# A vision block with a state scan, on one core: wider products on GpSimd, small steps moved to other engines, slots planned anew

## The reference, cut to what matters

```python
xb = silu(causal_conv4(x @ in_proj_w[:512].T)); z = x @ in_proj_w[512:].T
dt, B, C = softplus(dt_w * p0 + dt_b), p[1:17], p[17:33]      # p = xb @ x_proj_w.T
dA = exp(dt * A);  xs = (xb * dt) * B                         # 512 channels x 16 states x 196 tokens
h[t] = dA[t] * h[t-1] + xs[t]                                 # associative_scan
y = sum_n(h[n] * C[n]) + xb * D
y = layernorm(y) * ln_g + ln_b
out = (y * silu(z)) @ out_w.T
```

## Time and profile before

| what | us |
|---|---|
| median of the 3 runs (5220.89 to 5222.7) | 5221.56 |
| the profiled execution | 5220.4 |
| its span, first to last instruction | 5218.4 |
| TensorE busy (92%) | 4818.3 |
| GpSimd busy (83%) | 4331.2 |
| VectorE busy (72%) | 3737.0 |
| ScalarE busy (71%) | 3699.1 |

### The profile page before, as it was taken

The page is one execution under the profiler, slowest core; times in us unless marked ns, Lnnn a source line. Parts: engine busy times, 40 slices in busy tenths (PEclk is TensorE's granted clock), DMA queues, the critical chain, the costliest instruction groups (busy, mean ns, idle before and its releaser), DMA issues. The chain is left out here.

```text
span 5218.4 us, 95840 instructions
## 1 busy us (share of the span) xinstructions
PE 4818.3 (92%) x33664; PEld 4253.9 (82%) x33664; DVE 3737.0 (72%) x7504; ACT 3699.1 (71%) x8898; POOL 4331.2 (83%) x3272
## 2 busy tenths in 40 slices
PE   4799999999999999999999999999999999999986
PEld 4678888888888888888888888888888888888776
DVE  3677777777777777777777777777777777777753
ACT  4687777777777777777777777777777777777741
POOL 4998888888888888888888898898898888888840
PEclk8899999999999999999999999999999999999986
DMA  4222222222222222222222222322222322322200
GB/s 98 61 62 65 65 64 65 68 61 64 68 62 64 70 62 62 70 61 63 67 62 64 70 62 62 71 61 62 72 60 61 76 59 59 76 59 59 67 17 25
DMA packets 730622, 329.01 MB, mean 63 GB/s; under 512 B 631542, under 2 KB 655392, under 8 KB 729888
## 3 DMA queue, kind: packets, MB, share of 16 engines
q1 hardware_dynamic: 730144, 322.89, 25.4%
HBM read 307.88 MB, written 14.90 MB: 62 GB/s over the span
## 5 line engine op out<-in xcount | busy, mean ns | idle before, releaser
L1087 DVE TENSOR_TENSOR_SCAN X<-dA,X 128x392 f32<-128x392 f32 x2048 | 1871.7, 956 | 727.2 <-POOL X L470 455.5
L470 POOL TENSOR_TENSOR X<-u,Bb 128x784 f32<-128x784 f32 x1024 | 1896.6, 1852 | 9.4 <-DMA Bb<-proj_rows 9.4
L480 POOL TENSOR_TENSOR X<-X,Cb 128x784 f32<-128x784 f32 x1024 | 1893.0, 1849 | 0.0
L890 ACT ACTIVATE dA<-dt,negA 128x195 f32<-128x195 f32 x4096 | 1512.4, 417 | 149.5 <-DVE X L1087 129.4
L597 PE MATMUL YB<-idn,X 128*98 128x128 f32 x8192 | 1108.3, 282 | 27.6 <-POOL X L480 27.6
L597 PEld LDWEIGHTS YB<-idn,X 128*98 128x98 f32 x8192 | 930.6, 132 | 63.5 <-POOL X L480 34.9
L717 PE MATMUL G<-hg,we 128*128 128x196 f32 x4096 | 739.1, 338 | 14.1 <-DVE hg L1203 14.1
L717 PEld LDWEIGHTS G<-hg,we 128*128 128x128 f32 x4096 | 714.2, 198 | 27.5 <-issue 19.6
L544 PE MATMUL YB<-win,idn 128*98 128x196 f32 x2176 | 444.1, 346 | 0.0
L689 PEld LDWEIGHTS G<-vs,pT 98*98 98x98 f32 x4096 | 391.6, 171 | 37.1 <-issue 34.3
L485 POOL TENSOR_TENSOR veps_att<-mv_att,epsc 98x2 f32<-98x2 f32 x64 | 12.5, 195 | 488.3 <-DVE mv_att L1096 488.3
(11 more groups left out here) (145 smaller groups left out, 7307.0 us busy)
## 6 DMA issues: line engine op xcount, KB each, us to landing
Bb<-proj_rows SPq DMA_DIRECT2D x256, 392.0 KB, 5.0
Cb<-proj_rows SPq DMA_DIRECT2D x256, 392.0 KB, 4.1
Gb<-gate_rows SPq DMA_DIRECT2D x64, 784.0 KB, 5.6
px<-in_x SPq DMA_DIRECT2D x1024, 36.8 KB
out<-ob SPq DMA_DIRECT2D x64, 196.0 KB
dtin<-proj_rows SPq DMA_DIRECT2D x64, 98.0 KB, 2.8
we<-in_w_e SPq DMA_DIRECT2D x1, 2048.0 KB
proj_rows<-pj SPq DMA_DIRECT2D x64, 25.3 KB
```

Of the source, the lines that this page charges most:

```text
L470: tt(X[(GROUPS * s + g) % RING][:], u[q % 2][:, c:c + 1, :].broadcast_to([P, NG, T]), Bb[:, NG * ng:NG * (ng + 1), :], ALU.mult).then_inc( ...
L480: tt(t[:], t[:], Cb[:, n0:n0 + NG, :], ALU.mult).then_inc(prod_ready, 1)
L890: last = go(dA[i % DRING][:, j, 1:T], dt_[q % 2][:, c, 1:T], ACT.Exp, scale=negA[:, c, n:n + 1])
L1087: v.tensor_tensor_scan(t, dA[i % DRING].rearrange("p n t -> p (n t)"), t, 0.0, ALU.mult, ALU.add).then_inc(scan_done, 1)
```

## The change

Products with B and C take eight states (`NW`) at once, 128 x 1568, in a ring of four tiles. The scan still goes by groups of four states, two to a tile. A product with C waits for both of its groups; the sums come at slot g+3. The gate of y goes to VectorE (`gate_y`), with `scale_y` writing in place in PSUM; the square goes to ScalarE; adding epsilon (at the end of `moments`) and the shift (`negative_mean`) go to VectorE, and only the power stays on GpSimd. All slots, the orders within a slot on all five queues and the assignment of uses to the shared banks are new. The fills are 3 matmuls an image instead of 17.

```diff
-RING = 6
+NW = 2 * NG
+WC = STATES // NW
+WIDES = IC * WC
+RING = 4
-AT_WARM = (5, 8, 9, 12, 13,)
-WARM = (4, 4, 4, 3, 2,)
-AT_LOAD = -39
+AT_WARM = (6, 11, 16, 6, 6,)
+WARM = (2, 0, 0, 0, 1,)
+AT_LOAD = -51
-AT_XPROJ_OUT = -14
-AT_PROJ_STORE = -12
-AT_DT_LOAD = -11
-AT_SOFT = -9
+AT_XPROJ_OUT = -15
+AT_PROJ_STORE = -23
+AT_DT_LOAD = -20
+AT_SOFT = -10
-AT_IN = -1
+AT_IN = -2
+AT_SUM = 3
-AT_B = (-4, -4, -1, -1,)
-AT_C = (-1, -3, 3, 0,)
+AT_B = (-15, -16, -14, -12,)
+AT_C = (-10, -7, -5, -6,)
-AT_Y_STD = 21
-AT_Y_NORM = 21
+AT_Y_STD = 19
+AT_Y_SHIFT = 20
+AT_Y_NORM = 22
-AT_Y3 = 25
-AT_OUT = 25
+AT_Y3 = 23
+AT_OUT = 26
+AT_FFN_SHIFT = 40
-AT_ATT_STD = 61
+AT_ATT_STD = 62
+AT_ATT_SHIFT = 62
-AT_GATE_STORE = 71
-AT_GATE_LOAD = 74
+AT_GATE_STORE = 61
+AT_GATE_LOAD = 63
...
-        X = [sb(f"X{i}", [P, NG, T]) for i in range(RING)]
+        X = [sb(f"X{i}", [P, NW, T]) for i in range(RING)]
...
+            def inputs(s, q, w):
+                c, n0 = w // WC, NW * (w % WC)
+                if w == 0:
                     pool.wait_ge(u_ready, s + 1)
                 if c == 0:
-                    pool.wait_ge(B_landed[ng], 16 * (s + 1))
-                after(pool, prod_used, GROUPS * s + g + 1 - RING)
+                    for ng in range(n0 // NG, (n0 + NW) // NG):
+                        pool.wait_ge(B_landed[ng], 16 * (s + 1))
+                after(pool, prod_used, GROUPS * s + 2 * (w + 1 - RING))
+                tt(X[(WIDES * s + w) % RING][:], u[q % 2][:, c:c + 1, :].broadcast_to([P, NW, T]), Bb[:, n0:n0 + NW, :],
                    ALU.mult).then_inc(xs_pool, 1)
+            def times_c(s, w):
+                n0 = NW * (w % WC)
+                pool.wait_ge(scan_done, 2 * (GROUPS * s + 2 * (w + 1)))
...
+                t = X[(WIDES * s + w) % RING]
+                tt(t[:], t[:], Cb[:, n0:n0 + NW, :], ALU.mult).then_inc(prod_ready, 1)
             def inverse_std(s, n):
-                pool.wait_ge(stats_step[n], 4 * (s + 1))
-                steps = 3 if n in shift else 2
-                tt(veps[n][:], mv[n][:, :, 1], epsc[:], ALU.add).then_inc(rstd_step[n], 1)
-                if n in shift:
-                    tt(shift[n][:], mv[n][:, :, 0], mone[:], ALU.mult).then_inc(rstd_step[n], 1)
-                pool.wait_ge(rstd_step[n], steps * (s + 1) - 1)
-                tt(rstd[n][:], veps[n][:], mhalf[:], ALU.pow).then_inc(rstd_step[n], 1)
-                if n in shift:
-                    pool.wait_ge(rstd_step[n], steps * (s + 1))
-                    tt(shift[n][:], shift[n][:], rstd[n][:], ALU.mult).then_inc(shifted[n], 1)
+                pool.wait_ge(veps_ready[n], s + 1)
+                tt(rstd[n][:], veps[n][:], mhalf[:], ALU.pow).then_inc(rstd_ready[n], 1)
...
-                    for s, q in at(AT_KSQ):
-                        pool.wait_ge(where["k"].drained, where["k"].count("k", s))
-                        tt(ka[:], ka[:], ka[:], ALU.mult).then_inc(ksq_ready, 1)
-                    for s, q in at(AT_Y3):
-                        pool.wait_ge(S.drained, S.count("turn_y", s))
-                        pool.wait_ge(S.drained, S.count("z", s))
-                        tt(y3[:], y3[:], zs[:], ALU.mult).then_inc(y3_ready, 1)
+                    for k in range(WIDES):
+                        for s, q in at(2 * k + AT_TIMES):
+                            times_c(s, k)
+                    for k in range(WIDES):
+                        for s, q in at(2 * k + AT_IN):
+                            inputs(s, q, k)
...
             def scale_y(s):
                 o = filled("turn_y", s)
                 for c in range(IC):
-                    last = go(y3[:, c, :], o[:, c // 2, (c % 2) * T:(c % 2 + 1) * T], ACT.Identity,
-                              scale=lng[:, c:c + 1], bias=lnb[:, c:c + 1])
-                last.then_inc(S.drained, 1)
+                    mine = o[:, c // 2, (c % 2) * T:(c % 2 + 1) * T]
+                    last = go(mine, mine, ACT.Identity, scale=lng[:, c:c + 1], bias=lnb[:, c:c + 1])
+                last.then_inc(y_scaled, 1)
...
+                    for s, q in at(AT_KSQ):
+                        act.wait_ge(where["k"].drained, where["k"].count("k", s))
+                        go(ka[:], ka[:], ACT.Square).then_inc(ksq_ready, 1)
...
+            def gate_y(s):
+                dve.wait_ge(y_scaled, s + 1)
+                dve.wait_ge(S.drained, S.count("z", s))
+                if s > 0:
+                    filled("out", s - 1)
+                v.tensor_tensor(y3[:].rearrange("p (a b) t -> p a (b t)", a=2), S.tile,
+                                zs[:].rearrange("p (a b) t -> p a (b t)", a=2), ALU.mult).then_inc(S.drained, 1)
+                dve.wait_ge(S.drained, S.count("turn_y", s))
+                dve.sem_inc(y3_ready, 1)
             def scan_group(s, g):
-                dve.wait_ge(xs_pool, GROUPS * s + g + 1)
+                dve.wait_ge(xs_pool, WIDES * s + g // 2 + 1)
...
+                dve.wait_ge(stats_step[n], 4 * s + 2 * BLK)
+                v.tensor_scalar(veps[n][:], mv[n][:, :, 1], LN_EPS, None, ALU.add).then_inc(veps_ready[n], 1)
+            def negative_mean(s, n):
+                dve.wait_ge(rstd_ready[n], s + 1)
+                v.scalar_tensor_tensor(out=shift[n][:], in0=mv[n][:, :, 0], scalar=-1.0, in1=rstd[n][:], op0=ALU.mult,
+                                       op1=ALU.mult).then_inc(shifted[n], 1)
```

More of the change, by code:

```diff
@@ L430, in step @@
                         spread_rows(s, dtin[:].rearrange("p (o t) -> p o t", o=1), 0, 1, dtin_landed)
+                    for s, q in at(AT_GATE_LOAD):
+                        spread_gates(s)
+                    for ng in range(GC):
+                        n0 = NG * ng
+                        for s, q in at(AT_C[ng]):
+                            after(sp, prod_ready, WIDES * s - WC + ng // 2 + 1)
+                            spread_rows(s, Cb[:, n0:n0 + NG, :], 1 + STATES + n0, NG, C_landed[ng])
+                    for s, q in at(AT_PROJ_STORE):
+                        store_proj(s)
+                    for s, q in at(AT_STORE):
+                        store_out(s)
                     for s, q in at(AT_LOAD):
@@ L1224, in step @@
                             scan_group(s, k)
+                    for s, q in at(AT_Y3):
+                        gate_y(s)
+                    for s, q in at(AT_MIX):
+                        token_mix(s)
+                    for s, q in at(AT_FFN_STATS):
+                        dve.wait_ge(where["v"].drained, where["v"].count("v", s))
+                        moments(s, "ffn", lambda k: rs[:, k, :])
+                    for s, q in at(AT_GATE_IN):
+                        gate_part(s, 0)
+                    for s, q in at(AT_MOE_NORM):
+                        after(dve, out_landed, 16 * s)
+                        normalise(s, "moe", lambda k: where["moeT"].tile[0:TB, k * D:(k + 1) * D], ob, where["moeT"].drained)
                     for n in range(UNITS):
@@ L1227, in step @@
                             attended(s, q, n)
-                    for s, q in at(AT_FFN):
-                        ffn_sum(s)
+                    for t, which in AT_TAPS.items():
+                        for s, q in at(t):
+                            taps(s, which)
+                    for s, q in at(AT_VALUES_OUT):
+                        add_value_bias(s, q)
+                    for s, q in at(AT_Y_SHIFT):
+                        negative_mean(s, "y")
+                    for s, q in at(AT_OUT_STATS):
+                        o = filled("out", s)
+                        moments(s, "out", lambda k: o[0:TB, k * D:(k + 1) * D])
+                    for s, q in at(AT_ACC_OUT):
+                        add_residual(s, q)
+                    for s, q in at(AT_FFN_SHIFT):
+                        negative_mean(s, "ffn")
+                    for s, q in at(AT_ATT):
+                        dve.wait_ge(where["AV3"].drained, where["AV3"].count("AV3", s))
+                        moments(s, "att", lambda k: att[:, k, :])
                     for p in range(PAIRS):
@@ L1232, in step @@
                             scale_pair(s, p)
+                    for s, q in at(AT_TOP2):
+                        gate_part(s, GIN)
+                    for s, q in at(AT_GATE_X):
+                        gate_x(s)
+                    for s, q in at(AT_FFN):
+                        ffn_sum(s)
+                    for s, q in at(AT_OUT_NORM):
+                        normalise(s, "out", lambda k: where["out"].tile[0:TB, k * D:(k + 1) * D], h1, where["out"].drained)
+                    for s, q in at(AT_Y_STATS):
+                        dve.wait_ge(y_drained, IC * (s + 1))
+                        moments(s, "y", lambda k: ysb[:, k, :])
+                    for s, q in at(AT_Z_OUT):
+                        gate_z(s)
                     for n in range(UNITS):
```

378 lines of the change are left out of this document (161 added, 217 removed).

## The result

The changed kernel takes 5257.68 us (5256.89 to 5259.69) beside 5222.13 us for the kernel before on the same chip, a ratio of 1.0065 with a 95% interval of 1.0048 to 1.0083. The forecast was 4845 and faster. The time lies in the range that was given, but on the slow side of the kernel before, where the first rival had put it. One execution of the kernel before with 3 fills, shown further on, fell to a mean clock of 0.717 and took 8208.65 us; it is left out of that kernel's time.

The account below looks back on a forecast made before the run. The prediction took TensorE, with GpSimd close behind, to bound the kernel: the period falls from 78.1 to 72.2 us, 5.9 over 64 periods is 378 us, so 5221 becomes 4843, say 4845. Range 4670 to 5400, the forecast's own 4683 to 5003.

Parts of the forecast that it names:

- the first rival: Small steps on VectorE wait for GpSimd's SBUF reads: 8 steps cost 12.5 us a period, 5340 us; chance 0.32.
- the VectorE paragraph: VectorE gains the gate of y, 0.97 us, and eight small steps, 1.4 together, making 60.6 us a period.
- scans have room: On VectorE, shift steps waiting for roots on GpSimd cost nothing; 5.4 us if the room is gone.
- the bounds: On GpSimd, a wide product takes doubled time, 3.62 us, with bounds of -3.2 and +4.0 us a period.
- Its own relief: GpSimd loses the gate of y, the square and small steps: work falls from 67.5 to 62.2 us a period.
- TensorE's account: TensorE's work of 67.0 us, with 1.2 us of fills and 4.0 idle, gives a period of 72.2 us.
- 4.0 us of idle time: TensorE idles as long per period as in the kernel before, 4.0 us.
- The fills: On TensorE, 14 of 17 filling matmuls leave, taking 5.9 of 7.1 us a period.
- the second rival: TensorE's clock falls from 0.98 to 0.94 with 14 matmuls fewer: period 75.1 us, 5030 us; chance 0.10.
- Bank S, B and C, the square: Bank S up to 2 us of TensorE idle time, waits for B at 0, the square 0.47 us on ScalarE.

Follow-up runs that it names:

- narrow steps: The changed kernel with each two-column epsilon and shift step on VectorE made as two one-column steps: 4584.91 us, ratio 0.878 to the kernel before.
- the narrow move: The kernel before with only the small norm steps moved to VectorE, each as two one-column steps: 5245.94 us, ratio 1.0043.

## Why the prediction was wrong

**The step that failed** is the VectorE paragraph: "five `veps` and three `shift` steps at 0.18 us ... 1.4 together". They took 13.1 us, and of the 11.7 us too many 10.9 came out in the period: 78.9 us, and 68.0 with narrow steps. I read the price of a small step from rows in which one input lies in PSUM, and costed the rest at nothing "because scans have room". The forecast held 0.50 of the chance against 0.32 for the rival that had the answer. The rows already told for it: `wv` at twice the rate, and a kernel in which no two-tensor operation of VectorE read both from SBUF. I counted that neither row showed such a pair against GpSimd as openness, where it was the reason for asking how the design came by it.

**The first rival** was right in mechanism and nearly in size: 12.5 us a period forecast, 13.1 - 1.4 = 11.7 measured, VectorE busy 71.5 us, 5258 us in its range of 5120 to 5560. That the sum came so near is luck, for it had half an instruction for each of eight steps. In truth three epsilon steps (y, att, out) wait 0, since GpSimd stands waiting for just these; four steps wait for the rest of the instruction in flight, as the rival said; and `shift_y` waits for a whole product more, 3.5 us. Two errors of opposite sign nearly cancel. The Trainium skill's page "SBUF — State Buffer", in the section "Who interferes with whom", says that a VectorE instruction in a 2-port mode and a GpSimd instruction shut each other out, that one with two SBUF inputs contends with a GpSimd instruction that reads SBUF, and that the one which issues first holds the pair of ports for the whole instruction. The runs agree on the exclusion, for `shift` by its two inputs and for `veps` if it runs in that mode, which no row shows, and do not agree on the order: four products that began after the step went before it, 8.52 us in all. The Trainium skill's page "VectorE: DVE Perf Modes" (Mode 2×_2P) wants for that mode an outermost dimension beyond one that is even, or odd and equal on both sides; that the one-column `veps` escapes (0.149 us) agrees with it.

**GpSimd** was sized well: 61.1 us a period against 62.2, the wide product 3.48 from start to start against 3.62 us, within the bounds. Its own relief is no gain in the old plan, as the narrow move shows.

**TensorE's account** gave 72.2 us, and without the failed step the period is 68.0, below the range of 69.7 to 74.7 that I gave the forecast itself. Two terms were off. I carried over 4.0 us of idle time; it is 1.0. And TensorE's busy time is 985.67 / 14.7 = 67.0 us at a clock of 1.00, not 68.2 at 0.98. The reason that I gave for keeping the 4.0 us was only that they were there before.

**The fills** were costed as work that leaves. In the old plan 14 fewer make the kernel slower by 1.3%, so this part of the argument was wrong for that plan; in the new one, without the long steps, 14 fewer are worth 3.5 us a period (71.5 to 68.0). The clock did fall, to 0.93, but not by the second rival's cause: it follows from VectorE's long steps and goes back to 1.00 when they are short, with 3 fills in both.

**Bank S, B and C, the square** cost what was said once the steps are short: no function table is loaded beyond before, no wait for B or C stands in the list, TensorE's wait for the gate at bank S is 0.4 us a period (4.7 in the changed kernel, behind the long steps), and ScalarE needs 57.8 us in the narrow version. VectorE needs 60.8 there, against 60.6.

What stays open: how the 12.2% between the kernel before and the narrow version are shared by wide products, the gate of y, the square and the new plan. The small steps and the fills were tried alone in the kernel before, and neither is a gain there; the others were not, since their slots hang together. Open too is what decides whether a waiting step gets in between two products.

## What to carry to other kernels

Before an elementwise step is moved from GpSimd to VectorE, look where its inputs lie: a step with two tensors in SBUF, or a two-column step with a single input there, waited for GpSimd's running instruction and at times for several after it, however small it was, and all of VectorE's queue waited with it. One-column steps with per-partition scalars, an input in PSUM, or leaving the step on GpSimd avoided it here. And in a profile look at the mean time of small groups against their size, since such a wait is booked as busy time.

## What the runs showed that I had not expected

- The wait can go through a gapless row of GpSimd instructions: 8.52 us for a 98 x 2 step beside five products of 1.84 us, and a kernel slower by 24% by eight such steps an image, of which four wait. Other steps got in at the first or second seam of such a row.
- Added waits on GpSimd, with one shift two slots earlier, made the kernel 8.4% faster (5258 to 4818 us), since they opened the gaps in which three steps ran in 0.15 to 0.16 us each.
- A GpSimd product of 1568 elements takes 3.52 us, and 3.48 from start to start, where two of 784 take 3.70 and 3.62.
- Three filling matmuls an image are worth 90 us of 4585, and seventeen cost 218 beside three.
